# A recommendation tower's embedding tile, stored field by field instead of sample by sample

## What is computed

```python
sd = jnp.einsum('bfd,bd->bf', sparse_values, dense_features)
ss = jnp.einsum('bfd,bgd->bfg', sparse_values, sparse_values)
pairs = ss[:, iu, ju]                       # the 325 pairs above the diagonal
z = jnp.concatenate([dense_features, sd, pairs], axis=1)
h = jnp.concatenate([z, r_dense_features], axis=1)
h = jnp.maximum(h @ W_top1 + b_top1, 0.0)   # 512 wide
h = jnp.maximum(h @ W_top2 + b_top2, 0.0)   # 256 wide
y = h @ W_top3
```

## Time and profile before

| | |
|---|---|
| median of 2 runs | 377.64 us (377.49 to 377.80) |
| the profiled execution | 375.83 us |
| its span, from the first to the last instruction | 374.0 us |
| TensorE busy in the span | 337.8 us (90%) |
| ScalarE busy | 187.7 us (50%) |
| GpSimd busy | 246.3 us (66%) |
| VectorE busy | 243.8 us (65%) |
| mean granted TensorE clock | 0.991 |

### The profile page before, as it was taken

How to read it: one execution, slowest core, us unless ns; L and a number is a source line. 1 busy time by engine, 2 the same in 40 slices (tenths; PEclk the granted TensorE clock), 3 DMA queues, 4 the chain that set the end, 5 groups by cost and what they waited for, 6 DMA issues and landing times.

```text
span 374.0 us, 14392 instructions
## 1 busy us (share of the span) xinstructions
PE 337.8 (90%) x6278; PEld 312.3 (84%) x6278; DVE 243.8 (65%) x727; ACT 187.7 (50%) x270; POOL 246.3 (66%) x263
## 2 busy tenths in 40 slices
PE   0777867997999999999999999999999999989986
PEld 0765756997899989998999889989999898978874
DVE  1999959985596649754977478664984497511121
ACT  2343725563564456373754466545637365364532
POOL 5777676777777777777777777777777777720000
PEclk9999989998999999999999999999999999999999
DMA  7999652346533653364435443365335533340000
GB/s 172 251 240 244 202 153 73 105 108 143 128 115 93 142 142 99 89 144 125 113 82 129 127 130 105 95 147 136 107 92 133 131 107 89 74 110 16 4 2 0
DMA packets 41115, 43.92 MB, mean 117 GB/s; under 512 B 25614, under 2 KB 29946, under 8 KB 41052
## 3 DMA queue, kind: packets, MB, share of 16 engines
q1 hardware_dynamic: 32844, 26.20, 27.3%
q0 software_dynamic: 8192, 16.79, 17.6%
q10 hardware_dynamic: 16, 0.01, 0.0%
HBM read 38.12 MB, written 4.85 MB: 115 GB/s over the span
## 4 chain that ended last, share of the span: by engine, by line
PE 75%; DVE 12%; ACT 6%; DMA 3%; issue 2%; SPq 0%; ACTq 0%; DVEq 0%
PE et_ps L571 36%; PE g_ps L590 12%; PE m_ps L545 10%; DVE one_hot L476 7%; PE et_ps L563 7%; PE m_ps L631 7%; DVE table_lo L465 3%; ACT et L390 2%; ACT et L398 2%; PE m_ps L640 2%; DMA idb<-ids_one_hot 2%; DMA et<-tbl_in 2%; PE et_ps L600 1%; DVE w_lo L461 1%; DVE w_hi L459 1%
## 5 line engine op out<-in xcount | busy, mean ns | idle before, releaser
L358 POOL DMA_INDIRECT rows<-tbl_in,idx x256 | 245.4, 959 | 83.4 <-issue 71.3
L476 DVE TENSOR_SCALAR one_hot<-idb,first_row 125x256 fp32r<-125x256 int32 x640 | 200.0, 384 | 61.3 <-DMA idb<-ids_one_hot 35.5
L571 PE MATMUL et_ps<-one_hot,table_hi 125*128 125x256 f32 x640 | 170.7, 302 | 20.9 <-DVE one_hot L476 20.8
L571 PE MATMUL et_ps<-one_hot,table_lo 125*128 125x256 f32 x640 | 163.0, 288 | 0.0
L571 PEld LDWEIGHTS et_ps<-one_hot,table_hi 125*128 125x128 f32 x640 | 125.5, 196 | 26.6 <-issue 14.8
L571 PEld LDWEIGHTS et_ps<-one_hot,table_lo 125*128 125x128 f32 x640 | 126.0, 197 | 0.0
L398 ACT COPY et<-et_ps 128x512 f32<-128x512 f32 x64 | 80.3, 1259 | 23.3 <-PE et_ps L563 22.7
L390 ACT COPY et<-et_ps 128x256 f32<-128x256 f32 x80 | 48.6, 728 | 56.4 <-PE et_ps L571 56.3
L590 PEld LDWEIGHTS g_ps<-et 128*27 128x27 f32 x4096 | 46.6, 104 | 20.7 <-ACT et L398 6.1
L590 PE MATMUL g_ps<-et 128*27 128x26 f32 x4096 | 56.4, 192 | 8.2 <-ACT et L398 4.7
L411 ACT COPY gram<-g_ps 128x416 f32<-128x416 f32 x32 | 29.5, 921 | 49.8 <-PE g_ps L590 45.5
(11 more groups left out here) (58 smaller groups left out, 205.8 us busy)
## 6 DMA issues: line engine op xcount, KB each, us to landing
idb<-ids_one_hot SPq DMA_DIRECT2D x40, 256.0 KB
gram_rows<-gram SPq DMA_DIRECT2D x28, 169.0 KB
rows<-tbl_in,idx POOLq DMA_INDIRECT x256
et<-tbl_in SPq DMA_DIRECT2D x6, 448.0 KB
xt<-dense_t SPq DMA_DIRECT2D x8, 128.0 KB, 2.5
raw<-tbl_in SPq DMA_DIRECT2D x2, 448.0 KB
gram<-tbl_in SPq DMA_DIRECT2D x2, 448.0 KB
zt_raw<-gram_rows SPq DMA_DIRECT2D x14, 48.0 KB
```

The lines of the kernel that those rows point to most:

```text
L358: nc.gpsimd.indirect_dma_start(out=rows[:, i % ROW_RING, n, :], out_offset=None, in_=tables[GATHERED[k]], in_offset=bass.IndirectOffsetOnA ...
L476: nc.vector.tensor_scalar(one_hot[0:KP, at % OH_RING, :], idb[0:KP, pair % ID_RING, n % 2, :], first_row[0:KP, 0:1], float(k), ALU.subtrac ...
L571: last = nc.tensor.matmul(ps[:, n % 2 * CH:(n % 2 + 1) * CH], part[0:KP, n, k, :], one_hot[0:KP, at % OH_RING, :], start=k == 0 and part i ...
```

## The change

The tile is laid out as 27 fields of 128 samples each, in place of 128 samples of 27 fields. The helper `et_fields` that all writers of the tile use (L381, L390, L398) gives runs of 128 neighbouring samples. The gram's operands, 27 and 26 neighbouring words before, now are words that lie 128 words (512 bytes) apart. Sizes, counts of instructions, their order and all waits stay.

```diff
         def et_fields(tile, f, n):
 
-            return et_tile(tile).rearrange("d (b f) -> d f b", f=FW)[:, f:f + n, :]
+            return et_tile(tile).rearrange("d (f b) -> d f b", f=FW)[:, f:f + n, :]
...
-                    e = et_tile(TILES * c + n // (G_STEPS // 2))
+                    e = et_fields(TILES * c + n // (G_STEPS // 2), 0, FW)
                     for i in range(GROUPS // G_STEPS):
                         grp = n * GROUPS // G_STEPS + i
                         for q in range(4):
-                            at, col = (32 * q + grp % 32) * FW, grp % G_GROUPS * F
-                            last = nc.tensor.matmul(g_ps[bank % 2][32 * q:32 * q + FW, col:col + F], e[:, at:at + FW],
-                                                    e[:, at:at + F], start=True, stop=True)
+                            at, col = 32 * q + grp % 32, grp % G_GROUPS * F
+                            last = nc.tensor.matmul(g_ps[bank % 2][32 * q:32 * q + FW, col:col + F], e[:, :, at],
+                                                    e[:, 0:F, at], start=True, stop=True)
```

## The result

The kernel after takes 427.93 us, the median of two runs (425.38 and 430.48), against 377.64 us: 1.133 times, interval 1.120 to 1.146. It is slower by 50 us, where I had forecast 393 us, slower by 15. (428 us lies inside the stated range, which reached to 430 for a rival's sake, but not in the 385 to 405 us of the forecast's own case.)

A forecast was written before the change was run, and what follows sets the result against it. TensorE's own work was taken to bound the kernel, GpSimd's 40.0 us a chunk close behind. 375.8 + 21 (strided gram reads) - 5.6 (faster copies) = 391.2 us profiled, 393 us as median forecast; stated range 371 to 430.

The forecast's parts named there:

- the forecast's own case: Strided gram reads cost TensorE a factor between 2 and 2.6, giving 385 to 405 us; chance 0.36.
- What bounds the kernel: Middle chunks: TensorE's own work sets the pace, 39.8 of 40.4 us busy, with GpSimd close behind.
- GpSimd's 40.0 us a chunk: Steady part: 32 gathers a chunk, one every 1.25 us, so TensorE cannot bring a chunk below 40.0 us.
- The relief: ScalarE's copies L398 and L390 write neighbours and end earlier, sparing TensorE waits: 5.6 us, or 4 if GpSimd binds.
- The stride: Gram L590 reads words 512 bytes apart: 15.6 ns a pair for 6.8, +0.35 us a step, +21 us over 60 steps.
- the middle of the two writes, 2.3 times: Price of TensorE's strided gram read, taken between ScalarE's strided SBUF writes at 2.1 and 2.5 times packed.
- the sum: Profiled execution: 375.8 + 21 for the gram's stride - 5.6 for the copies = 391.2 us.
- The four groups queue for their words: Rival at the gram: 21.8 ns a pair or more, +44 us, 416 us (502 at 44.5 ns); chance 0.26.
- A strided read costs nothing: Rival at L590's read of `et`: zero to 0.2 us a step, leaving the gain, 373.6 us; chance 0.34.
- eight fetches a nanosecond: Argument against free strided reads: 53 separate fetches in 6.8 ns are eight a nanosecond out of each partition.
- The Trainium skill's rule: A 16-byte SBUF line needs two hits for full bandwidth: gram's new operands not free; supports the side, no size.

The follow-up runs named there:

- best: Kernel before with its layout, ScalarE's embedding copies and L411 walking so they write short runs of neighbours and read PSUM strided: 371.78 us against 376.49, 0.987.
- writes_only: Kernel after with its field-by-field copies, but both gram operands read packed (wrong words): 373.72 us against 376.46 before, ratio 0.990.
- pad132: Kernel after with fields 132 words (528 bytes) apart in place of 128, one-hot ring 10 in place of 12: 385.04 us against 380.35 before.
- step4: Kernel before, both gram operands read with a step of 4 words (16 bytes), other words: 389.39 us against 376.49 before.
- the skewed samples: Kernel after, four column groups reading samples 16 or 64 bytes apart in place of 128: 389.6 and 390.15 us against 376.49 and 376.46 before.

## Why the prediction was right or wrong

**What bounds the kernel: right.** In the middle chunks TensorE's own work set the pace before and does so after (47.07 busy of 47.07 us); in the second phase after, GpSimd's gathers hold part of the chain. GpSimd's 40.0 us a chunk is the floor that `best` and `writes_only` come down to.

**The relief: right.** L398 at 606 and L390 at 375 ns (618 and 370 forecast), the wait down to 1 us, and for this half alone 2.7 us less than before by the medians and 4.0 by the ratio (1.5 to 6.4 by its interval), where 4 were forecast. After the change the copies beside a gram burst lose this again, but nearly all of them are off the chain.

**The stride: right in side, wrong in size.** The step that failed is "I take the middle of the two writes, 2.3 times", together with its silent premise, that the four groups stay beside each other at any address. The 2.3 came from ScalarE's writes, and no row of before had a strided read by TensorE. In its place there are two costs. A word alone in its 16 bytes lengthens a round from 27 to some 50 ns (1.8 to 1.9 times, `pad132`, `step4`), a little less than 2.3. And four groups that read at a distance of 128 bytes, each with 512 bytes from word to word, meet at one bank (inferred, as said), which lengthens the round from 50 to 92 ns (3.4 times in all). 53 words in 23.1 ns are 0.44 ns a word (0.43 in the expectations). The second cost had no place in the sum, and without it (`pad132`) the kernel takes 385 us, less than my forecast.

The sum with the measured sizes: 60 steps x (1.71 - 0.77) = +56.4 us, waits for L398 6.1 to 1.0 = -5.1, transposes that wait for rows +3.9: +55.2 us, against +54.7 between the two spans (428.7 and 374.0). TensorE's busy time says the same: 337.8 to 394.1 is +56.3, and its idle time went from 36.2 to 34.6 us. The chain gives L590 only 42 us more, since in the second phase it runs through gathers while the gram goes on beside them. The profiled execution is the slower of the two timed ones.

**The rivals.** "The four groups queue for their words" was the nearest, with 21.8 ns a pair and 416 us; it had 0.26. Its mechanism was half right: they queue, but not at a common port. Then the skewed samples would queue as well, and they don't. What the runs fit is a queue at a bank, both operands together at 0.44 ns a word, not one operand at 0.84. That the two prices are close is chance. "A strided read costs nothing" holds for a step of 8 bytes only, of those tried. My argument against it, eight fetches a nanosecond, was not the point either: with padding the same fetches take 12.7 ns.

**The Trainium skill's rule** of two hits a line ("SBUF — State Buffer", Specifications (TRN2)) chose the right side, and the runs bear it out with a size: 7.0 ns a pair with two words a line, 13.0 with one. The Trainium skill says on the same page, in "Who interferes with whom", that TensorE and ScalarE "never wait on anyone". The measurement differs: L446 on one partition has 1276 ns in place of 416.

**Not forecast at all** was that others stand still during the bursts. By the sum it adds only the 3.9 us of late rows. Single gathers took far longer than any one gram burst, the longest 11.92 us. The bursts are not all of the reason, as `best`, where nothing is stalled, has one of 5.52 us too (after first):

```profile
73.52 11.92 POOL L358 DMA_INDIRECT rows<-tbl_in,idx  x1 [2.73 <-PE et_ps L563]
```

```profile
68.49 5.52 POOL L358 DMA_INDIRECT rows<-tbl_in,idx  x1 [1.28 <-PE et_ps L564]
```

Both, and the one of 6.92 us, end within 0.9 us after an unbroken run of VectorE's instructions does (84.62, 73.88 and 101.27 us), which points at VectorE. But many gathers pass beside such runs in 0.95 us, and no run changed VectorE's work alone, so the cause stays open.

## What to carry to other kernels

Before changing a layout so that one engine writes neighbours, see who reads it and at what rate: here nearly 60 us off an engine that was half idle (ScalarE 187.7 to 129.1 us in `writes_only`) bought 3 us, and the strided reads of the full engine cost 56. If TensorE must read single words with a stride, take care that the stride of 512 bytes and groups 128 bytes apart don't come together: moving either one away took off most of the loss, and one word of padding a field was worth 43 us. And look first whether the order in which a copy walks is enough, as it was here: let it write short runs of neighbours and read PSUM with the stride.

## What was not expected of the hardware

- Column groups fetch beside each other: one group alone takes 27.4 ns for a pair of 27 and 26 packed float32 columns, four in turn 6.8 ns a pair.
- While TensorE's four groups queue for one place of SBUF, most of the other engines' instructions stall: two L441 1.95 us in place of about 0.9, a 1x256 copy 1.30 us in place of 0.42, a cast of VectorE 2.85 in place of 0.49. L411, which writes single words 256 bytes apart, does not (0.86 us). With one operand strided or the groups skewed, when a pair takes 14 to 15 ns, the stall is all but gone (ScalarE busy 130.6 to 133.0 us, 129.4 with padding).
- ScalarE writes runs of 2, 4 and 16 float32 words at 485 ns for 256 elements, 675 for 512 and 507 for 416, where single words had taken 728, 1259 and 921; these times include its reads of PSUM with a stride.
